# A cross-attention and mixture-of-experts block on one Trainium2 core: rows scattered to an expert-sorted table, VectorE block transposes, double-buffered sums

## The reference, cut to what matters

```python
# x (4, 1024, 1024), ctx_512 (4, 1024, 256), W (8, 1024, 1024), all fp32
def xattn(ctx, adj, W, b):                 # D = 256
    si, sj = ctx @ W[0, :D], ctx @ W[0, D:]
    return 0.6 * sigmoid(si[:, :, None] + sj[:, None, :] + b) + 0.4 * adj
def ffn(x, wg, W, b):                      # 4096 tokens, 8 experts, top 1
    probs = softmax(x @ wg); idx = argmax(probs); gate = probs[idx]
    return gate * (x @ W[idx].T + b[idx])
x = x + tanh(g_xattn) * xattn(ctx_512, layernorm(x), L0_xattn_W, L0_xattn_b)
x = x + tanh(g_ffn) * ffn(layernorm(x), L0_ffn_wg, L0_ffn_W, L0_ffn_b)
```

## Time and profile before

| | |
|---|---|
| time, median of 3 runs | 717.78 us (717.33 to 719.3) |
| span of the profiled execution | 716.3 us |
| busy PE / DVE / ACT / POOL | 632.9 / 369.2 / 286.0 / 279.0 us |
| DMA | 110 MB, mean 154 GB/s |
| chain that ended last | PE 65%, issue 13%, POOL 10%, DVE 6% |

### The profile page before, as it was taken

One profiled execution on the slowest core, in us unless ns is written; L12 is line 12 of the kernel. 1 busy time (PEld: TensorE's weight loads), 2 busy tenths in 40 slices (PEclk: granted clock), 3 DMA queues, 4 the chain that ended last, 5 costly groups with the idle time before them and its releaser, 6 DMA issues.

```text
span 716.3 us, 14295 instructions
## 1 busy us (share of the span) xinstructions
PE 632.9 (88%) x3516; PEld 513.3 (72%) x3517; DVE 369.2 (52%) x646; ACT 286.0 (40%) x454; POOL 279.0 (39%) x428
## 2 busy tenths in 40 slices
PE   6778777778369998998999999999999999999992
PEld 4555565656258787787888878878887888888881
DVE  4776766764996335534633653553364337333341
ACT  3977667766245213323422432332153125222220
POOL 3777787787640231223122222322312321222231
PEclk9999999999769999999999999999999999999997
DMA  6777776697049334614722561461353222222110
GB/s 214 218 257 236 228 220 217 186 342 269 3 160 395 115 118 158 207 60 118 288 73 84 159 238 60 157 254 60 112 199 134 91 87 60 77 101 85 38 60 6
DMA packets 35265, 109.97 MB, mean 154 GB/s; under 512 B 8448, under 2 KB 8576, under 8 KB 35200
## 3 DMA queue, kind: packets, MB, share of 16 engines
q1 hardware_dynamic: 23152, 75.74, 30.9%
q0 software_dynamic: 12048, 33.64, 14.1%
HBM read 79.41 MB, written 35.72 MB: 161 GB/s over the span
## 4 chain that ended last, share of the span: by engine, by line
PE 65%; issue 13%; POOL 10%; DVE 6%; ACT 2%; POOLq 1%; DMA 1%; DVEq 1%; SPq 0%; ACTq 0%
PE bank L1071 53%; PE bank L1021 7%; POOL ln_rs L395 4%; PE bank L1056 4%; POOL ln_rs L393 2%; POOL ln_rs L398 2%; DVE wt L747 2%; POOL ln_b L402 1%; DVE lane_hot L835 1%; DMA gates<-in_L_xattn_b 1%; POOL x_in L406 1%; PE bank L947 1%; ACT wt L576 1%; DVE unused L668 1%; POOLq L386 1%
## 5 line engine op out<-in xcount | busy, mean ns | idle before, releaser
L1071 PE MATMUL bank<-wt,xt_hi 128*128 x1152 | 367.8, 400 | 6.0 <-DVE wt L747 6.0
L1071 PEld LDWEIGHTS bank<-wt,xt_hi 128*128 128x128 f32 x1152 | 207.5, 189 | 44.9 <-issue 9.2
L1071 PE MATMUL bank<-wt,xt_lo 128*128 x576 | 225.8, 392 | 0.0
L592 ACT ACTIVATE xt_hi<-bank 128x512 fp32r<-128x512 f32 x74 | 44.2, 598 | 262.5 <-PE bank L1071 262.5
L1071 PEld LDWEIGHTS bank<-wt,xt_lo 128*128 128x128 f32 x576 | 108.2, 188 | 23.5
L476 POOL COPY scatter_row<-slot_row 128x1 uint32 x36 | 6.5, 180 | 291.0 <-DVE res L883 185.2
L869 DVE TENSOR_TENSOR xt_lo<-bank,xt_hi 128x512 fp32r<-128x512 f32 x74 | 51.0, 691 | 124.6 <-ACT xt_hi L592 124.6
L747 DVE TENSOR_TENSOR wt<-bank,wt 128x512 f32 (+1 forms) x128 | 84.1, 686 | 39.6 <-ACT wt L576 30.0
L879 DVE TENSOR_TENSOR res<-bank,bias_bc 128x512 f32<-128x512 f32 x72 | 49.4, 686 | 103.8 <-PE bank L1071 71.5
L576 ACT ACTIVATE wt<-bank 128x512 f32 (+1 forms) x128 | 73.3, 598 | 73.5 <-PE bank L1021 73.5
L1021 PE MATMUL bank<-ident,w_raw 128*128 128x128 f32 x512 | 75.6, 282 | 8.4 <-DVE wt L747 8.4
(11 more groups left out here) (132 smaller groups left out, 554.5 us busy)
## 6 DMA issues: line engine op xcount, KB each, us to landing
w_raw<-in_L_ffn_W SPq DMA_DIRECT2D x64, 512.0 KB, 6.2
x_in<-in_x SPq DMA_DIRECT2D x32, 512.0 KB, 4.2
x_rows<-x SPq DMA_DIRECT2D x32, 512.0 KB, 4.8
ctx_in<-in_ctx SPq DMA_DIRECT2D x8, 512.0 KB, 5.5
bias_bc<-in_L_ffn_b SPq DMA_DIRECT2D x8, 512.0 KB, 5.0
x_gat<-x_rows,gather_row POOLq DMA_INDIRECT x39, 4.4
meta_gat<-tok_rows,gather_row POOLq DMA_INDIRECT x39, 3.4
out_x<-res,scatter_row POOLq DMA_INDIRECT x36, 3.4
```

The costliest lines, as they stand in the source:

```text
L592: nc.scalar.activation(xt_hi[:, KH * g:KH * (g + 1), :].rearrange("p k n -> p (k n)"), xt_ps[g][:, :], ACT.Copy).then_inc(xt_hi_ready[g], 1)
L1071: last = nc.tensor.matmul(out_ps[h][:, :], xs[:, k, :], wt[:, bass.ds(par, 1), part, k, HALF * h:HALF * (h + 1)] .rearrange("p a o -> p (a ...
```

## The change

The kernel is rewritten in most places; the products of the slots stay the same in number and kind.

- **Tile stage, unrolled.** Tiles stand in a ring of 16, `xr`, with 16 more columns for each row's own scalars (token, sum of squares, sum of tanh, mean, variance, eight logits). The sigmoid is written as a tanh. Group scalars are made once per four tiles (`norm_scalars`). Both context sums come from TensorE (`sum_context`). The router's stationary operand is now the transposed tile, so that logits come out by token (`route`). `xt_ps` alternates between two PSUM pairs. ScalarE copies one half of the transposed tile and VectorE the other.
- **Routing by groups of four tiles.** `choose`, `rank` and `position` give each row of the group its place in `table`, which has 4096 rows of room for each expert; GpSimd scatters each tile's rows there (`store`, 4160 bytes a row), a group behind.
- **Slots.** The slots of an expert are 128 rows in succession from `table`; the last ones overlap what came before, and `beyond` keeps doubled rows from being written. `load_rows` loads them twice: in blocks (`xb`) for the transpose and by rows (`rows`). ScalarE issues these five DMAs.
- **Transposes of weights and rows** are VectorE block transposes of 32 x 32 from SBUF to a PSUM pair; the DMAs bring in runs of 256 columns to the partition block that makes the whole a transpose. A piece is 128 output columns x 1024; eight per expert, four held in `w_raw`. All stand in the slot of kind 2 and alternate between `cut_a` and `cut_b`.
- **Sums.** Rows are multiplied before they are normalised; mean, gate and bias are brought in afterwards: `slot_scalars` on GpSimd, `exp_sum` and `scaled_bias` on ScalarE, and `finish` as one pass of 1024 columns. Sums alternate between two PSUM pairs (`out_ps[r % 2]`), and the rows' parts between two buffers. GpSimd scatters `rows` to the output.

```diff
-            tiles(0, 0, first=True)                       # TensorE, tile stage
-            with pe.Fori(1, CTX_LOOPS // 2) as ii:
...
+            for g in range(3):
+                turn_context(g)
+                sum_context(g)
+            pe.wait_ge(wg_landed, 16)
+            for t in range(T):
+                g, r = t // GR, t % GR
+                if t:
+                    route(t - 1)
+                turn_tile(t)
+                if r == 0 and g + 3 < NG:
+                    turn_context(g + 3)
+                if r == 1 and g > 0:
+                    rank(g - 1)
+                if r == 2 and g + 3 < NG:
+                    sum_context(g + 3)
...
+            def store(t):                                 # GpSimd
+                s = slot_of(t)
+                pool.wait_ge(pos_ready, t // GR + 1)
+                pool.wait_ge(tok_ready, t // GR + 1)
+                pool.wait_ge(sq_ready, t + 1)
+                nc.gpsimd.indirect_dma_start(
+                    out=table, out_offset=bass.IndirectOffsetOnAxis(ap=pos[:, t:t + 1], axis=0),
+                    in_=xr[:, s, :], in_offset=None,
+                    bounds_check=E * N - 1, oob_is_err=False).then_inc(row_stored[s], 16)
...
+        def load_rows(engine, row0, u, first):
+            for q in (0, 2, 1, 3):
+                engine.dma_start(xb[32 * q:32 * (q + 1), first % 2, :, :],
+                                 in_blocks(table[bass.ds(row0, P), :], q)).then_inc(xb_landed[first % 2], 16)
+            engine.dma_start(rows[:, first % RING, :], table[bass.ds(row0, P), :]).then_inc(
+                rows_landed[first % RING], 16)
...
+            for s in range(RX):                           # SyncE, behind the tiles
+                sp.wait_ge(row_stored[s], 16 * (T // RX))
+            load_rows(sp, 0, 0, 0)
...
+            def slot_scalars(u, n, k):                    # GpSimd, slot loop
+                settled(rows_landed[k], 16 * n + 16)
+                nc.gpsimd.tensor_scalar(scal[:, k, 0:1], rows[:, k, SQ:SQ + 1], 1.0 / H, EPS,
+                                        ALU.mult, ALU.add).then_inc(var_ready, 1)
...
+                settled(var_ready, u + 1)
+                nc.gpsimd.tensor_tensor(scal[:, k, 2:3], scal[:, k, 0:1], minus_half[:, 0:1],
+                                        ALU.pow).then_inc(rstd_ready, 1)
...
+                settled(rec_ready, u + 1)
...
+                settled(rb_ready, u + 1)
+                nc.gpsimd.tensor_tensor(rows[:, k, 0:H], rows[:, k, 0:H], rb[:, :], ALU.add).then_inc(base_ready, 1)
...
+                        slot_scalars(t + 1, i + (r + 1) // RING, (r + 1) % RING)
+                        settled(finished, t + 3)
...
+                    with act.If(kind > 1):                # ScalarE, slot loop
...
+                        exp_sum(t + 1, (r + 1) % RING)
+                        settled(summed, t + 1)
+                        for m in range(4):
+                            cut_high(e + 1, m, nxt, (cut_b, cut_a)[m % 2])
+                        ahead()                           # scaled_bias(t + 1), next_rows(t + 3)
+                        settled(summed, t + 2)
+                        xt_high(t + 2, r, cut_b)
+                        for m in range(4, K):
+                            cut_high(e + 1, m, nxt, (cut_a, cut_b)[m % 2])
...
+            def turn_weights(e, m, ps):                   # VectorE
+                if m > 1:
+                    dve.wait_ge(w_ready, K * e + (m if m == 4 else m - 1))
+                dve.wait_ge(w_landed[m % WR], 128 * e + 64 * (m // WR) + 64)
+                nc.vector.transpose(turned(ps), blocked(w_raw[:, m % WR, :, :])).then_inc(w_turned, 1)
...
+                    with dve.If(kind > 1):                # VectorE, slot loop
...
+                        turn_weights(e + 1, 0, cut_b)
+                        dve.wait_ge(xt_ready, t + 2)
+                        turn_weights(e + 1, 1, cut_a)
+                        cut_low(e + 1, 0, nxt, cut_b)
+                        turn_weights(e + 1, 2, cut_b)
+                        cut_low(e + 1, 1, nxt, cut_a)
+                        one_over(t + 1, (r + 1) % RING)
+                        turn_weights(e + 1, 3, cut_a)
+                        cut_low(e + 1, 2, nxt, cut_b)
+                        dve.wait_ge(w_ready, K * e + K + 3)
+                        turn_rows(t + 2, 2 * i + (r + 2) // 2, r % 2, cut_b)
+                        cut_low(e + 1, 3, nxt, cut_a)
+                        finish(t, r)
+                        turn_weights(e + 1, 4, cut_a)
+                        xt_low(t + 2, r % 2, cut_b)
...
+                        cut_low(e + 1, 7, nxt, cut_b)
+                        settled(w_ready, K * e + 2 * K)
...
+                            one_over(t + 1, (r + 1) % RING)      # ordinary slot
+                            dve.wait_ge(xt_ready, t + 2)
+                            turn_rows(t + 2, 2 * i + (r + 2) // 2, r % 2, cut_a)
+                            finish(t, r)
+                            xt_low(t + 2, r % 2, cut_a)
...
+            def multiply(t, r, e, par):                   # TensorE
+                pe.wait_ge(xt_ready, t + 1)
+                pe.wait_ge(finished, t + 1)
                 for h in range(2):
-                    pe.wait_ge(w_lo_ready, G * e + G // 2 * (h + 1))
-                    pe.wait_ge(res_ready[h], t)
-                    if h == 1:
-                        turn(t + 1)
+                    pe.wait_ge(w_ready, K * e + K // 2 * (h + 1))
```

1338 lines of the change are left out of this document (582 added, 756 removed).

## The result

The changed kernel takes 761.83 us (median of 4 runs, 758.3 to 767.45) against 717.56 us before (717.12 to 719.3): ratio 1.062, interval 1.057 to 1.067. It is slower, by 44 us, where 22 us less were forecast. The profiled execution has a span of 765.8 us, against 716.3 before and 694.4 in the sum of the prediction. This execution is the longest of the four runs (767.45 us).

What follows compares the result with a forecast made beforehand. The loop before was taken as TensorE's. Slot 0's end 229.5 + products 382.6 + waits 51 + code 18 + closing 13.3 = 694.4 us of span, plus 1.5 gives 696 us, 3.0% less than 717.8; range 660 to 725.

Steps and rivals of the forecast that it cites:

- VectorE's 4.55 us a tile: Tile stage: VectorE's work per tile sets the pace, 31 x 4.55 from 34 us, last addition at 188.
- the circle I gave TensorE: Tile stage, five context groups: copy, router (1.9), transposes (1.1) and copy form a circle, 2.6 us more per group.
- Contexts: Tile stage: 4 us of context work between two tiles in five groups adds 13 us in all.
- From the last addition to the end of slot 0: Routing and slot 0: first product 26 us after the last addition, slot 0 ending 41.5 after it, at 229.5.
- chain from the last cut to the low rows: Slot loop, change of expert: after VectorE's last cut, scalars, bias, five DMA issues and rows follow; slot start at C + 8.9.
- third slot behind each preparing one: Slot loop: TensorE waits 5 to 8 us there for the low rows, and nowhere else but at turns of the loop.
- the 9 us that I gave slot 0's own preparation: Slot loop: slot 0's preparation adds 9 us of TensorE waiting to 42 from later ones, together 51.
- The code stalls: Slot loop: VectorE idles with nothing to wait for at turns of its loop; 18 us taken, bounds 0 and 90.
- A: Rival, slot loop: chains are shorter than thought and TensorE stays the bound, 627 us; chance 0.22.
- B: Rival, slot loop: VectorE's transposes are slow, 68 us per microsecond of price, 771 us at 2.3 us each; chance 0.11.
- C: Rival, slot loop: code stall at every slot of the longer bodies, 3 us showing in 30 slots, 768 us; chance 0.14.
- D: Rival, tile stage and routing: routing saves as promised and the tile stage doesn't grow (176); 12 us less, inside the range.

Runs made afterwards that it cites:

- the wide router: Changed kernel with the router's products streaming 96 columns in place of 8, same logits twelve times: 720.3 us, ratio 1.002.
- the order with the later choice: Changed kernel, contexts' loads a group earlier, 8-column router, TensorE's transposes before the previous tile's router, experts chosen one tile later: 725.1 us, ratio 1.011.
- slot 0 let in early: Changed kernel with VectorE letting TensorE into slot 0 as soon as that slot's rows are cut: 764.9 us, ratio 1.067.
- the two orders on ScalarE: Changed kernel with ScalarE's ordinary-slot order changed: scaled bias, high part of rows, loads, 756.5 us; or high part, bias, loads, 780.0 us.
- no weights: Changed kernel without loads, transposes and cuts of experts 1 to 7's weights; all products use the first expert's: 705.3 us, ratio 0.983.
- the later choice: Changed kernel, contexts loaded earlier, 96-column router, ScalarE's row loads last; plus transposes before the previous tile's router, experts chosen one tile later: 666.0 us, ratio 0.926.
- the loads on SyncE: Changed kernel with contexts loaded earlier, 96-column router, bias and rows first on ScalarE; plus SyncE issuing each slot's row loads: 655.7 us, ratio 0.914.
- the pieces loaded beside the scatters: Changed kernel, contexts earlier, 96-column router, ScalarE's loads last; plus weight pieces 4 to 6 loaded before slot 0's rows, slot 0 opened early: 674.6 us.
- bias, rows, loads: Changed kernel with ScalarE, in an ordinary slot, making scaled bias, then high part of rows, then issuing the five loads: 756.5 us, ratio 1.056.

## Why the prediction was wrong

**The step that failed: "VectorE's 4.55 us a tile" as the pace of the tile stage.** Last addition forecast at 188, measured at 258. VectorE's own work was sized well: at the high clock with the contexts in time, the stage goes at 4.47. What failed is the circle I gave TensorE, with durations from the earlier trace rows, rows of the high clock. The changed router streams 8 columns where the old one streamed 128, TensorE's clock stayed at its lower level through the stage but for stretches behind the context sums, and the circle of router, transposes and copy became 6.23 us. 31 x (6.23 - 4.55) = 52 of the 70 us. That it was the clock is shown by the wide router, which does the same work with the clock up. The terms that I listed for VectorE add up to 4.35 and not 4.55, which changes nothing in this. The Trainium skill, "TensorE: Matmul & The Clock Gate", part 1, has the gate follow how busy TensorE has been. By the busy column this kernel's TensorE, at 191 of 224 us, was busier than before (120 of 153.5), and the order with the later choice showed 50 of 50 at 0.50, with 96 columns 40.4 of 50 at 1.00. The measurement decides: the clock did not follow the busy time that the profile counts.

**Contexts.** I took 13 us for them and overlooked the queue: SyncE's reloads of x wait for scatters, with the contexts' loads behind them. The three waits alone are 15.4 us, and taking them away gave 19. With the work for them the 20 tiles with contexts took 29 us more than 20 circles, 16 over the forecast; tile 0 came 5.4 us late, as the first context groups ran at a mean clock of 0.56; and 3.4 us come off again, as the last addition runs ahead of TensorE's last tile. That is the other 18 of the 70. Some 5 of the 70 are this execution's own: in four kernels with the same tile stage (slot 0 let in early, the two orders on ScalarE, no weights) the last addition starts at 250.2 to 252.0, not at 256.7.

**From the last addition to the end of slot 0** 60 us, forecast 41.5. Four things: router and transposes at the low clock, 4.6 more (8.7 against 4.1); VectorE's waits for weight piece 4, whose loads stand behind slot 0's rows on SyncE, and for slot 1's rows, 3.3 + 2.3; slot 0 at the low clock, 14.0 us in place of 10.9; and its first half, 5.5 us, which I had ahead of the pieces and which the gate on `finished` holds until behind them. That is 18.8. The last of them costs nothing in the end: in the run that opened the gate it came back as a wait ahead of slot 3.

**Right: everything in the slot loop but the code.** VectorE's transpose 1.25 us (taken 1.2), row addition 2.39 (2.4), chain from the last cut to the low rows 8.6 (8.9), round of an ordinary slot 8.3 (9.1), third slot behind each preparing one as the place of the waits (TensorE resumes there 52.2, 52.2, 61.9, 53.7, 62.0 and 63.0 us apart; forecast 51.7 for four slots, 60.8 for five), no waits elsewhere but two of 1.4 and 2.0. Behind slot 0's end the loop lasts 434 us: 382.6 and 51.4, where 51 was forecast. But that agreement is partly luck: 37.8 are waits and the other 13.6 are what slots lose at the low clock behind them, which I did not have at all. And the 9 us that I gave slot 0's own preparation were 0.5 (the wait ahead of slot 3), since slot 0 itself was late. The run without weights shows that all of it belongs to the change of expert.

**The code stalls** of 5 us did not come on VectorE: forecast 18 us, measured 6.4 of idle time with nothing to wait for ahead of the preparations, at most 1.2 at a time, and 9.9 ahead of the reciprocal that follows them, 1.5 to 1.9 at a time, where my chain had 0.8. ScalarE shows 26.7 us ahead of the exponential, up to 4.5, but part of that is a wait: at 359.37 the scalar that it needs was ready at 356.7. What a stall costs there was not tested; VectorE waits 1.4 us for ScalarE's first cut at that place and 0.4 in slot 0. So the 18 us are too much in the sum. My reading was short as well: the trace before has such a stall at all eight turns of VectorE's loop (4.8 to 6.1 us), not at five.

Together: 70 + 18.5 - 17.6 + 0.5 = 71.4, the distance from 694.4 to 765.8.

**The rivals.** A (products without gaps) is seen only without the weights. B's price was wrong, 1.25 us. C at its full price, 768, would give about the right time by the wrong mechanism: no stall stands ahead of most slots. D (no growth of the tile stage) is the opposite of what happened. None of my rivals had the clock or SyncE's queue in the tile stage.

**What stays open:** why the later choice doesn't add to the loads on SyncE, what the pieces loaded beside the scatters delay, and how the gain of the loads on SyncE divides.

## What to carry to other kernels

Durations of TensorE from a trace hold only at that row's clock: when a change makes its products narrower, work the sum out at both levels, and look at the clock column of the stage before anything else. The repair may cost nothing; here 96 columns took as long as 8. When a queue's order is touched, list what each issue in it waits for and who stands behind it, and when an issue is moved on an engine that has work in every slot, count it in the whole distance between two changes, not only in the chain where it shows.

## What was not expected of the hardware

- TensorE without a pause for 50 us at a granted clock of 0.50, with fp32 products of 8 moving columns and transposes of 128; the same order with 96 columns at 1.00, though busy for 40.4 of 50 us.
- Sixteen router records with a full stationary tile take 3.55 us at the low clock with 8 as with 96 columns, and at the high one 2.02 and 2.00 us.
- Behind a wait of 5 to 6 us between slots the clock is at 0.50 for some 5 us, and the next slots lose 1.5 to 2.8 us more. Behind single waits of 2.02 and 1.44 us a slot took 11.19 and 11.16 us, with no such loss. The length of the wait alone doesn't tell: with bias, rows, loads a slot took 11.18 us behind a wait of 3.47, and 12.78 behind one of 2.67.
